# Three triangle layers and a Mamba layer on one core: gate products in front of the bias addition, reordered ends

## The reference

```python
# layers L0, L1, L2, x is (1, 256, 256, 32), HID is 64, window 4
xn    = _ln(x, norm_scale, norm_bias)
left  = (xn @ Wl + bl) * mask * _sigmoid(xn @ Wlg + blg)
right = (xn @ Wr + br) * mask * _sigmoid(xn @ Wrg + brg)
og    = _sigmoid(xn @ Wog + bog)
out   = _banded_ingoing(left, right, 4)          # 9 diagonals beside the main one
out   = _ln(out, out_norm_scale, out_norm_bias) * og
x     = x + (out @ Wo + bo)
# layer L3: Mamba over the rows, 64 inner channels, 16 states
h = exp(dt * A) * h + dt * B * x ; y = h . C ; y = (y + xc * D) * silu(z) ; y @ W_out
```

## Time and profile before

| | us |
|---|---|
| median of 3 runs | 2895.09 |
| runs, lowest and highest | 2893.14 and 2897.2 |
| the profiled execution | 2893.14 |
| its span, first to last instruction | 2891.3 |
| TensorE busy | 2320.9 |
| VectorE busy | 2326.4 |
| ScalarE busy | 1856.1 |
| GpSimd busy | 2051.8 |

### The profile page before, as it was taken

How to read it: one execution, slowest core, us unless ns; L and a number is a source line. 1 busy time by engine, 2 the same in 40 slices (tenths; PEclk the granted TensorE clock), 3 DMA queues, 4 the chain that set the end, 5 groups by cost and what they waited for, 6 DMA issues and landing times.

```text
span 2891.3 us, 37834 instructions
## 1 busy us (share of the span) xinstructions
PE 2320.9 (80%) x13030; PEld 733.9 (25%) x13030; DVE 2326.4 (80%) x2039; ACT 1856.1 (64%) x2534; POOL 2051.8 (71%) x1194
## 2 busy tenths in 40 slices
PE   4889778897788977478787887878878788887886
PEld 1343112441124321122222222222222222222221
DVE  5655556655557445399999999999999999999998
ACT  3624556345573445378777787777877778777773
POOL 2544234552346422289999999999999999999998
PEclk9999989999999989799999999999999999999998
DMA  4797315984239866667777677777776777777765
GB/s 160 252 333 243 102 51 164 358 282 122 70 120 323 285 201 170 146 168 180 186 169 184 174 180 185 173 185 176 180 186 168 184 174 180 188 169 186 177 172 124
DMA packets 257692, 537.26 MB, mean 186 GB/s; under 512 B 39592, under 2 KB 150960, under 8 KB 256608
## 3 DMA queue, kind: packets, MB, share of 16 engines
q1 hardware_dynamic: 226448, 466.99, 59.4%
q0 software_dynamic: 19040, 64.24, 7.6%
q10 hardware_dynamic: 12016, 3.61, 0.6%
HBM read 395.41 MB, written 139.33 MB: 185 GB/s over the span
## 4 chain that ended last, share of the span: by engine, by line
DVE 24%; issue 17%; ACT 10%; PE 6%; POOL 1%; ACTq 0%; DVEq 0%; POOLq 0%
DVE m_hs L539 12%; DVE m_pb L534 12%; ACT m_da L476 4%; PE m_pb L340 2%; ACT L424 1%; ACT L406 1%; ACT m_act L412 1%; PE m_misc L272 1%; PE m_py L314 1%; PE m_py L307 1%; ACT m_act L418 1%; POOL m_hs L552 1%; ACT m_xg L390 0%; PE m_misc L254 0%; ACT m_cs L454 0%
## 5 line engine op out<-in xcount | busy, mean ns | idle before, releaser
L552 POOL TENSOR_TENSOR m_hs<-m_hs,m_cs 128x1024 f32<-128x1024 f32 x512 | 1200.0, 2357 | 128.4 <-DVE m_hs L539 84.5
L539 DVE TENSOR_TENSOR_SCAN m_hs<-m_da,m_pb 128x1024 f32<-128x1024 f32 x416 | 951.1, 2286 | 14.4
L340 PE MATMUL m_pb<-m_dtx,late 64*128 64x512 f32 x1664 | 498.7, 672 | 234.1 <-DVE m_hs L539 226.8
L534 DVE TENSOR_TENSOR m_pb<-m_pb,m_bs 128x1024 f32<-128x1024 f32 x416 | 502.7, 1208 | 14.0 <-PE m_pb L340 13.7
L476 ACT ACTIVATE m_da<-m_dtb,m_a_neg 128x1020 f32<-128x1020 f32 x414 | 464.3, 1143 | 4.4 <-DMA m_dtb<-dt_rows 2.4
L1557 POOL TENSOR_TENSOR t_xc<-t_xc,big 128x512 f32<-128x512 f32 x96 | 120.0, 1270 | 315.4 <-DVE big L1437 315.3
L340 PEld LDWEIGHTS m_pb<-m_dtx,late 64*128 64x128 f32 x1664 | 154.8, 199 | 553.7 <-DVE m_hs L539 318.7
L314 PE MATMUL m_py<-m_hs,late 128*32 128x512 f32 x2048 | 275.9, 611 | 4.7 <-POOL m_hs L552 4.7
L1440 DVE SCALAR_TENSOR_TENSOR t_xc<-t_bank,t_vec,t_xc 128x512 f32<-128x512 f32 x96 | 72.1, 751 | 208.2 <-PE t_bank L1122 208.2
L1318 ACT ACTIVATE t_sq<-t_bank 128x512 f32<-128x512 f32 x192 | 106.1, 596 | 197.4 <-PE t_bank L1169 197.0
L1554 POOL TENSOR_TENSOR t_sq<-big 128x512 f32<-128x512 f32 x96 | 102.9, 1082 | 182.3 <-ACT big L1300 108.8
(11 more groups left out here) (168 smaller groups left out, 3785.7 us busy)
## 6 DMA issues: line engine op xcount, KB each, us to landing
m_dtb<-dt_rows SPq DMA_DIRECT2D x510, 512.0 KB, 5.8
late<-right_factor POOLq DMA_DIRECT2D x102, 512.0 KB, 6.4
right_factor<-t_tile SPq DMA_DIRECT2D x192, 256.0 KB, 4.0
t_tile<-band_out SPq DMA_DIRECT2D x183, 256.0 KB, 4.0
band_out<-t_vwin SPq DMA_DIRECT2D x48, 512.0 KB
band_out<-t_vwin SPq DMA_DIRECT2D x48, 480.0 KB
dt_rows<-m_dt SPq DMA_DIRECT2D x64, 256.0 KB, 4.7
t_xc<-in_x_cm SPq DMA_DIRECT2D x4, 2048.0 KB, 14.6
```

Source lines behind the costliest of these rows:

```text
L340: m = nc.tensor.matmul(pb[s % 2][:, half(n)], spread[rows, dg, :], dtx[par][rows, half(q)], start=True, stop=True)
L534: nc.vector.tensor_tensor(products, products, bs[q][:, :], ALU.mult).then_inc(u_done, 1)
L539: nc.vector.tensor_tensor_scan(hs[:, g % H_RING, :], decays, products, 0.0, ALU.mult, ALU.add).then_inc(h_ready, 1)
L552: nc.gpsimd.tensor_tensor(hs[:, g % H_RING, :], hs[:, g % H_RING, :], cs[q][:, :], ALU.mult).then_inc(hc_ready, 1)
```

## The change

It has six parts.

1. **Output part.** VectorE takes the gate products (`a3`) in front of the y2 addition, and the statistics move from the end of a step to behind the next step's bc3 product.
2. **Start.** x is loaded in eight parts in place of four. SP waits for the seventh before it loads the layer's weights, and ScalarE before it issues the third and later constants.
3. **Banks at a layer's end.** The bc3 of units 26 to 31 write banks 4, 5, 7, 0, 1, 4 rather than 7, 3, 7, 1, 4, 5.
4. **Hand-over.** GpSimd no longer issues rows 128 to 160. ScalarE issues them, and pieces move between ScalarE and SP with other waits.
5. **Preparation of the Mamba layer** moves into the end of the last triangle block.
6. **End.** The last product by C and the last gate product are done by VectorE, the latter straight from PSUM, and the last four stores are split between SP and ScalarE.

```diff
         def bc3_bank(n):
-            return (7, 3)[n % 2] if n < 28 else (7, 1, 4, 5)[n - 28]
+            return (7, 3)[n % 2] if n < 26 else (4, 5, 7, 0, 1, 4)[n - 26]
...
-                for part in range(4):
-                    o = 16 * COLS * part
-                    sp.dma_start(xc[:, BAND + o:BAND + o + 16 * COLS], w["x_cm"][:, o:o + 16 * COLS]).then_inc(x_loaded[part], 16)
+                size = 2 * HALFROWS * COLS // X_PARTS
+                for part in range(X_PARTS):
+                    o = size * part
+                    sp.dma_start(xc[:, BAND + o:BAND + o + size], w["x_cm"][:, o:o + size]).then_inc(x_loaded[part], 16)
+                sp.wait_ge(x_loaded[X_PARTS - 2], 16)
...
+                sp.wait_ge(x_stored[2], 16 * 4 * 4)
+                hand_over(sp, first_row(24, 0), first_row(28, 0))
+                hand_over(sp, first_row(24, 1), first_row(28, 1))
                 sp.wait_ge(x_stored[3], 16 * 4 * 4)
                 hand_over(sp, first_row(28, 0), first_row(16, 1))
...
+                pe.wait_ge(shared.w_in, 16 * len(shared.weights))
+                pe.wait_ge(free[2], use[LAYERS - 1, "y1", 2 * UNITS - 1])
+                nc.tensor.matmul(bank[2][:, 0:P], shared.by_name["wx_dt"][:, :], shared.by_name["w_dt"][:, :],
+                                 start=True, stop=True).then_inc(wdt_ready, 1)
...
-                for dst, name in const_loads:
+                for i, (dst, name) in enumerate(const_loads):
+                    if i == 2:
+                        a.wait_ge(x_loaded[X_PARTS - 2], 16)
                     a.dma_start(dst[tuple(slice(None) for _ in dst.shape)], w[name]).then_inc(consts, 16)
...
-                a.wait_ge(x_stored[2], 16 * 4 * 4)
-                hand_over(a, first_row(24, 0), first_row(28, 0))
                 a.wait_ge(x_stored[1], 16 * 4 * 8)
+                hand_over(a, P, first_row(24, 0))
+                a.wait_ge(x_done, 2 * UNITS * (LAYERS - 1) + 28)
                 hand_over(a, first_row(16, 1), first_row(24, 1))
...
                 a.wait_ge(x_stored[3], 16 * 4 * 4)
-                hand_over(a, first_row(24, 1), ROWS)
+                hand_over(a, first_row(28, 1), ROWS)
...
-                        for n in st["y2"]:
-                            v.wait_ge(full[3], use[l, "y2", n])
-                            nc.vector.scalar_tensor_tensor(x_unit(n), bank[3][:, :], vec32[:, 2:3], x_unit(n),
-                                                           ALU.add, ALU.add).then_inc(free[3], 1)
+                        for n in STEPS[s - 1]["bc3"] if s else ():
+                            unit_stats(l, n)
                         split = 1
                         for t in st["band"][:split]:
                             band(l, t)
...
                                 nc.vector.tensor_tensor(tile[:, slot, :], bank[p][:, :], gate_slot(at[l, "open", n, p]),
                                                         ALU.mult).then_inc(free[p], 1)
+                        for n in st["y2"]:
+                            v.wait_ge(full[3], use[l, "y2", n])
+                            nc.vector.scalar_tensor_tensor(x_unit(n), bank[3][:, :], vec32[:, 2:3], x_unit(n),
+                                                           ALU.add, ALU.add).then_inc(free[3], 1)
...
-                            if l == LAYERS - 1 and n in (26, 27):
-                                g_.wait_ge(x_stored[1], 16 * 4 * 8)
-                                hand_over(g_, P, first_row(24, 0), (2 * n - 52, 2 * n - 51), shared.x_in_pool)
...
+                v.wait_ge(h_ready, end)
+                nc.vector.tensor_tensor(hs[:, (end - 1) % H_RING, :], hs[:, (end - 1) % H_RING, :], cs[1][:, :], ALU.mult).then_inc(last_c, 1)
+                v.wait_ge(hc_used, end)
...
+                nc.vector.tensor_tensor(gated[:, half(1)], py[1][:, :], act[par][:, W + HALF:W + 2 * HALF], ALU.mult).then_inc(y_gated, 1)
```

## The result

The changed kernel takes 2926.21 us (median of 5 runs, 2921.63 to 2929.63) where the kernel before takes 2895.09. The ratio is 1.0103, with a 95% interval of 1.009 to 1.0117: slower by 31 us. The direction was forecast and the price of the main step nearly so, but the time is outside the range of 2889 to 2921. The profiled execution took 2924.59 us with a span of 2922.8, against 2891.3 before, so the traces have to account for 31.5 us. In all that follows one execution is left out of the ratios: of e6 one took 3246.2 us at a mean granted clock of 0.644, where its other nine have 0.938 to 0.948.

A forecast was written before the change was run, and what follows sets the result against it. TensorE was taken to bound the first three layers, VectorE the Mamba layer. Terms 39 - 7 - 2 - 6.4 - 1.3 - 8.5 - 3 plus 0.5 gave +11.5 on 2895.09, so 2906 us, range 2889 to 2921.

The forecast's parts named there:

- 0.5 us of remainders: Unspecified small items, added to the sum of the terms, +11, to give +11.5 us.
- Band steps: Nine steps in each of layers 1 to 3: the third band waits 1.95 us for bank 3, together +39 us.
- three pairs in a layer and layer 3 partly waiting for tiles: Output steps without bands: gate products first save 0.95 us per pair of steps, together -7 us.
- the additions end some 4 us sooner: End of layer 3: GpSimd no longer issues copies between its last additions, some 4 us of the 8.5 us gain.
- From layer 3 to Mamba: Hand-over between these layers: additions end sooner and Mamba preparation goes behind the copies, -8.5 us (-5 to -10.5).
- the rival in which the hand-over gains nothing: Layer 3 to Mamba: same bytes at the same rate, so 8.5 us less gain, 2915 us; chance 0.09.
- Start: Loading of x and constants up to the first matmul: less statistics after the last landing, -1.3 us (-0.5 to -2.5).
- Layers 1 and 2 without the band steps: Output steps, bc3 steps and layer ends of layers 1 and 2: forecast -13.3 us.
- End: End of the program: VectorE does the last products, stores are split two and two, -3.0 us (-2 to -4).
- The clock rival: Band steps: TensorE's new gaps lower its clock, 51 us on top, 2957 us; chance 0.05.
- The rival of waits hidden behind transfers: Band steps: transfers hide part of the waits, band term 29 us, time 2896 us; chance 0.19.
- that of a faster kernel: Transfers limit the band steps, later bands cost nothing and the other gains remain, 2867 us; chance 0.10.

The follow-up runs named there:

- e6: As e2, with GpSimd's eight copies issued behind its last addition, not between the additions of units 18 to 25: 2891.03 us, ratio 0.9983.
- e1: The kernel before with one edit, the y2 addition behind the gate products in every step: 2932.68 us, ratio 1.0136.
- e2: The changed kernel with the y2 addition back in front of the first band in steps that have bands: 2884.6 us, ratio 0.9964.
- e3: As e2, but with the y2 addition between the first band and the gate products in band steps: 2892.92 us, ratio 0.9999.
- e9: As e8, with the eight early copies issued by SP right after its last tile load, not by GpSimd: 2874.33 us, ratio 0.992.
- e10: As e8, with two of the four copies between units 18 and 21 held back to units 22 and 23: 2876.72 us, ratio 0.9932.
- e5: As e2, and in layer 3 the y2 addition is first in every step: 2886.39 us, ratio 0.9963.
- e11: As e8, with GpSimd's copy of unit 20 issued after the addition of unit 21: 2875.39 us, ratio 0.993.
- e4: The kernel before with the new start alone, x in eight parts and later loads behind the seventh: 2892.24 us in one run.
- e8: As e2, with SP and ScalarE going on to weights and constants after the fourth part of x, not the seventh: 2878.06 us, again 2881.65.

## Why the prediction was wrong

The forecast was 11.5 us more, and the traces have 31.5. Of these 20 us, 12 are in layer 3, 4.3 on the way from layer 3 to the Mamba layer, 3.9 in layers 1 and 2, 3.1 at the start and 2.8 in the band steps; 5.5 us in the body of the Mamba layer go the other way. For the 0.5 us of remainders in the forecast no run shows a source.

**Band steps: right.** The third band waits for bank 3, which the addition now frees behind the gate products. Forecast were 1.95 us for each of 27 steps, some of it absorbed by waits for tiles, in sum 39; measured were 1.8 us for each and 41.8 in sum. e1, e2 and e3 show it with all, none and a third of the wait. The absorption went as assumed, with the steps that also have variance matmuls at 8.94 us, not 8.81.

**The step that failed** is the one on layer 3 behind its bands, in the prediction's words *"three pairs in a layer and layer 3 partly waiting for tiles"* and *"the additions end some 4 us sooner"*. Gains of some 2 and 4 us were booked there as if the tiles came no later than before. In fact layer 3 outside its band steps lost 6 us, 12 us off the forecast. The second gain came, 3.3 us: from GpSimd's addition of unit 25 to its last it takes 14.9 us and not 18.2. But the waits for tiles in layer 3 grew from 16.9 to 27.1 us, and units 25 and 26 took 7.2 us more. The earlier trace rows was read for the hand-over and the earlier trace rows for the band steps, and neither for the tiles that are loaded while GpSimd's copies run. e6, e9 and e10 show that the copies are the cause. The stores of x, which layers 1 and 2 do not have either, were not tried by themselves. Why the tiles came later here than in the kernel before, which has the same early copies, was not settled: e1 shows that the order alone does it, e5 that the other edits do it without that order, and e11 that the place of the third copy accounts for a part.

**From layer 3 to Mamba: mis-sized**, and nearly right only by luck in a sum with what follows. Of the 8.5 us, 4 were the additions above. The other 4.5, the preparation that moved ahead, gave 0.2: VectorE starts on x 21.4 us after the last addition, not 21.6, because it now waits for a copy, with 2.22 us of idle time that the copy ends. *"The bytes are the same"* had been noted against the gain, and the trace bears it out; the rival in which the hand-over gains nothing, priced at 2915 us, came nearer here than the forecast. That the whole from the last addition to the end is -8.7 us, against -7.5 forecast, comes from 5.5 us in the body of the Mamba layer, for which nothing was forecast and which are within its spread.

**Start: wrong in sign**, by 3.1 us. *"The constants are issued after the seventh part lands"* was right, and so was *"TensorE needs them all"*; the price was wrong. The last constant was issued by 25.36 and released TensorE at 31.71. A landing of some 3 us had been assumed, without a row for it. From the last issue to the release it was 6.4 us. e4 and e8 confirm the place.

**Layers 1 and 2 without the band steps: mis-sized.** -9.4 rather than -13.3. The wait of 2.48 us at the layer's end is gone, as forecast, but it was counted with its consequences at 3.2 us, and part of the gain in the steps without bands was taken back where ScalarE computes its inverse roots. Units 21 and 22 took 1.8 us more in layer 1 and 1.0 in layer 2, which is 2.8 of the 3.9 us that are missing. TensorE waited there for squares, which ScalarE takes up only after the roots (timeline of the changed kernel, layer 1):

```profile
360.12 1.08 ACT L1303 ACTIVATE t_sq<-t_bank 128x512 f32<-128x512 f32 x2
360.75 1.29 DVE L1448 TENSOR_TENSOR t_tile<-t_bank,t_gate 128x512 f32<-128x512 f32 x2 [4.74 <-ACT t_sq L1303]
361.08 0.60 ACT L1271 COPY big<-t_bank 128x512 f32<-128x512 f32 x1
361.35 1.94 PE L1123 MATMUL t_bank<-t_sq,t_var 128*32 128x512 f32 x8 [3.79 <-ACT t_sq L1303]
```

**End: right**, -3.0 as forecast.

**The other rivals.** The clock rival did not come. Over nine steps with a gap of 1.8 us each the granted clock is 1.00 (2.4 GHz), as the window above shows. The Trainium skill, "TensorE: Matmul & The Clock Gate", section "A second HAM failure mode: psum-queue depth-cycling", describes short idle times between groups of matmuls that make the clock swing; in the trace of the changed kernel gaps of 1.8 us in every step did not do this. e1, with the same gaps, had one fall of the clock in its 27 band steps, which cost 1.6 us there. A fall in a band step is not tied to the gaps either: e8, without them, has one too (granted clock 0.97 over the nine steps of layer 2). The rival of waits hidden behind transfers needed the band term at 29 us, and that of a faster kernel under 28; it was 41.8.

## What to carry to other kernels

When instructions of one engine change places, list for each which resource it frees and who is next to fill that resource; here an addition moved by three places held a bank that TensorE wants 0.95 us after its former release, in 27 steps. A gain in a stage whose loads run beside bulk copies is worth less than the same gain in a stage without them: price it by the waits for transfers of that very stage. And here a bulk copy belonged behind the last small load that somebody waits for: that, the addition in front of the bands and the earlier constants made a kernel of 2874 us (e9) out of the one of 2926, 0.8% under the one before. A sum that comes out right over a long stretch should be split before it is believed: here 5.5 of 8.7 us lay where nothing had been changed.

## What the runs showed of the hardware that was not expected

A tile load of 256 KB that was issued beside four copies of 512 KB took over 9 us to release its matmul (issued from 1172.94, released at 1182.10), where 4.0 us is the median of these loads on the page. In every kernel in which GpSimd issues its eight copies between its additions, the eighth was issued 6.2 to 8.6 us after GpSimd was ready for it, with nothing in the profile that it waited for. In the kernel before that is 13.7 us after the fifth copy (1162.41 and 1176.08), in the changed one 13.5 (1205.87 and 1219.38). Where all eight stand together (e6), seven were issued in 7.4 us and the eighth 20.2 us later. On SP eight such copies took 19.8 us to issue. What holds these issues was not tried by itself.
